# First stage of a two-layer kernel: token rows spread by a load, values in 16 columns a head, feed-forward ahead of the first rotation

## The reference, cut to what matters

```python
xn = layernorm(x)
# attention, 16 heads of 8
Q, K = rope(xn @ W_q.T), rope(xn @ W_k.T)
V = xn @ W_v.T
# feed-forward whose weights depend on the batch: tokens 1 to 16 of it
even, odd = xn[:, 1:17][:, ::2], xn[:, 1:17][:, 1::2]
m1 = (even[:, :4, :, None] * odd[:, :4, None, :]).reshape(B, 512, 128)
m2 = (even[:, 4:, :, None] * odd[:, 4:, None, :]).reshape(B, 128, 512)
h = gelu(xn @ W1.T + scale * (xn @ m1.T) + b1)
u = h @ W2.T + scale * (h @ m2.T) + b2
```

## Time and profile before

| | |
|---|---|
| median of 3 runs | 987.8 us (986.38 to 988.86) |
| the profiled execution | 987.3 us |
| its span | 985.5 us |
| mean granted clock of TensorE | 0.943 of full |
| PE, DVE, ACT, POOL busy | 88%, 81%, 74%, 29% of the span |
| first stage | up to about 121 us |

### The profile page before, as it was taken

The page is one execution under the profiler, slowest core; times in us unless marked ns, Lnnn a source line. Parts: engine busy times, 40 slices in busy tenths (PEclk is TensorE's granted clock), DMA queues, the critical chain, the costliest instruction groups (busy, mean ns, idle before and its releaser), DMA issues. The chain is left out here.

```text
span 985.5 us, 25281 instructions
## 1 busy us (share of the span) xinstructions
PE 862.6 (88%) x9414; PEld 461.0 (47%) x9414; DVE 801.8 (81%) x1697; ACT 726.1 (74%) x1493; POOL 290.6 (29%) x329
## 2 busy tenths in 40 slices
PE   3999999999999999999899899898999999899960
PEld 3666533333333333333334776543444444377750
DVE  6665899999999999999842664599999999847885
ACT  2656438888888888888876555688999999867741
POOL 4866311111111000000003676501444442014560
PEclk9999959999999999999989899879999999989985
DMA  5579681644445353330007778595544442556717
GB/s 170 200 262 338 253 210 50 209 101 113 113 102 120 86 124 77 75 67 23 14 8 185 234 243 247 138 232 117 119 110 91 99 80 47 136 187 185 225 75 255
DMA packets 119385, 140.92 MB, mean 143 GB/s; under 512 B 20109, under 2 KB 82138, under 8 KB 118624
## 3 DMA queue, kind: packets, MB, share of 16 engines
q1 hardware_dynamic: 113888, 127.45, 47.5%
q0 software_dynamic: 5376, 11.85, 4.1%
HBM read 77.63 MB, written 63.25 MB: 143 GB/s over the span
## 5 line engine op out<-in xcount | busy, mean ns | idle before, releaser
L974 ACT ACTIVATE probsB<-psB 128x512 f32<-128x512 f32 (+2 forms) x640 | 310.1, 565 | 75.9 <-PE psB L1029 49.3
L174 DVE TENSOR_REDUCE mxB<-psB 128x1 f32<-128x512 f32 x428 | 245.9, 642 | 9.2 <-PE psB L151 8.1
L1022 PE MATMUL psB<-q_groups,k_groups 64*128 64x512 bf16 (+3 forms) x768 | 206.4, 332 | 17.1 <-DVE mxB L174 8.3
L151 PE MATMUL psB<-k_groups,q_groups 64*128 64x512 bf16 (+2 forms) x740 | 205.6, 338 | 1.8 <-PEq L408 1.8
L1050 PE MATMUL psB<-probsB,vB 128*32 128x512 f32 (+3 forms) x1536 | 165.8, 504 | 0.7 <-ACT probsB L974 0.5
L1862 ACT ACTIVATE psD<-psD 128x896 f32<-128x896 f32 (+2 forms) x192 | 153.5, 800 | 9.2 <-PE psD L1916 8.7
L1022 PEld LDWEIGHTS psB<-q_groups,k_groups 64*128 64x128 bf16 x768 | 67.8, 94 | 162.7 <-ACT probsB L974 140.2
L1791 DVE TENSOR_REDUCE sumsD<-psD 128x1 f32<-128x128 f32 (+3 forms) x256 | 113.3, 482 | 7.0 <-PE psD L1939 4.9
L1916 PE MATMUL psD<-k_groups,q_groups 64*128 64x512 bf16 (+3 forms) x384 | 103.3, 343 | 14.1 <-ACT psD L1862 3.4
L174 DVE TENSOR_REDUCE mx2B<-psB 128x2 f32<-128x256 f32 (+3 forms) x188 | 102.6, 596 | 11.0 <-PE psB L158 9.5
L1029 PE MATMUL psB<-hide_laterB,chooseB 64*128 64x64 bf16 (+1 forms) x1024 | 109.8, 205 | 0.0
(11 more groups left out here) (240 smaller groups left out, 1552.5 us busy)
## 6 DMA issues: line engine op xcount, KB each, us to landing
v<-vaugA SPq DMA_DIRECT2D x4, 2048.0 KB, 8.8
vB<-v SPq DMA_DIRECT2D x16, 512.0 KB
q_groups<-q SPq DMA_DIRECT2D x32, 200.0 KB
k_groups<-k SPq DMA_DIRECT2D x32, 200.0 KB
back<-emptyB POOLq DMA_DIRECT2D x16, 256.0 KB, 3.8
q<-hiA SPq DMA_DIRECT2D x12, 256.0 KB, 6.5
k<-hiA SPq DMA_DIRECT2D x12, 256.0 KB, 5.8
q_groups<-q SPq DMA_DIRECT2D x32, 96.0 KB
```

Source lines behind the costliest of these rows:

```text
L151: ins = nc.tensor.matmul(bank[:, to:to + w], self.q[r, s, a, t * P:t * P + P], self.k[r, s, a, HALF * c:HALF * c + w], start=True, stop=(c ...
L174: return nc.vector.tensor_reduce(dst, src, AX.X, ALU.max)
L974: nc.scalar.activation(probs[:, n % DEEP, 0:w], st[n % BANKS][:, 0:w], ACT.Exp, scale=DH ** -0.5).then_inc(exp_done, 1)
L1022: ins = nc.tensor.matmul(bank[:, to:to + w], k[half[r], s, hq // 2, jt * P:jt * P + P], q[half[r], s, hq // 2, i0:i0 + w], start=True, sto ...
```

## The change

- `pick`, its load and PE's `outer` go. In `normalise`, after the second tile, ACT stores the eight rows to memory (`first`, 4 KB), and in a new step `spread_first` it waits for that and loads them back with a broadcasting access into all 128 partitions of `firstA` (512 KB written). DVE's `weights` waits for this load (`first_moved`) and reads `firstA` in SBUF where it read PSUM banks 0 and 1.
- `spread_first(0)` stands between `normalise(0)` and `columns(0)`; `spread_first(b+1)` between `second_part(b, 0)` and `second_part(b, 1)`.
- A head's values take 16 columns (`VC`) in `vaug`, `v0` and the tile of `attention`, whose products still take 32 columns: the head's own 16 and the 16 behind them. The tile gets 16 spare columns, set to zero by POOL.
- In batch 0, DVE does `weights(0)` before `rope(0, 0)`, ACT does `gelu(0, 0)` before `first_part(0, 0)`, and PE does `project(0, 1)` in the middle of `feed_forward(0, 0)`. ACT runs a small Gelu at its start.

```diff
+VC = 2 * DH
-        pick = m.sb("pickA", [P, 8, P])
+        first = m.sb("firstA", [P, 8 * D])
-        vaug = m.sb("vaugA", [P, 2, NT, H, VW])
+        vaug = m.sb("vaugA", [P, 2, NT, H, VC])
...
-        consts = [(ident, A["ident"]), (w_proj, A["w_proj0"]), (pick, A["pick"]), (cos, A["cos0"]), (sin, A["sin0"]),
+        consts = [(ident, A["ident"]), (w_proj, A["w_proj0"]), (cos, A["cos0"]), (sin, A["sin0"]),
...
-                    dve.wait_ge(outer_done, b + 1)
+                    dve.wait_ge(first_moved, 32 * (b + 1))
...
-                        V.scalar_tensor_tensor(w1e[:, c], ps[:, 0, c], odd[:, j:j + 1], w1[:, c], ALU.mult, ALU.add)
+                        V.scalar_tensor_tensor(w1e[:, c], first[:, c], odd[:, j:j + 1], w1[:, c], ALU.mult, ALU.add)
...
-                    rope(b, 0)
                     if b == 0:
                         weights(b)
+                    rope(b, 0)
...
+                        if t == 1:
+                            act.wait_ge(xn_ready, NT * b + 1)
+                            act.dma_start(A["first"][b].rearrange("o (j c) -> (o j) c", c=D), xn[1:17:2, 0, :]).then_inc(first_moved, 16)
+
+                def spread_first(b):
+                    act.wait_ge(first_moved, 32 * b + 16)
+                    if b:
+                        act.wait_ge(w_ready, b)
+                    act.dma_start(first[:, :], A["first"][b].broadcast_to((P, 8 * D))).then_inc(first_moved, 16)
...
+                act.wait_ge(ready, 1)
+                nc.scalar.activation(warm[:, :], eps[:, :], ACT.Gelu)
                 normalise(0)
+                spread_first(0)
                 columns(0)
...
                     keep_v(b)
+                    gelu(b, 0)
                     if b == 0:
                         first_part(0, 0)
-                    gelu(b, 0)
...
                     second_part(b, 0)
+                    if b + 1 < B:
+                        spread_first(b + 1)
                     second_part(b, 1)
...
+                    if b == half == 0:
+                        pe.wait_ge(terms_ready, 1)
+                        project(0, 1)
...
                 turn_rows(0)
-                outer(0)
                 pe.wait_ge(xnT_ready, 2)
                 project(0, 0)
                 values(0)
-                pe.wait_ge(terms_ready, 1)
-                project(0, 1)
...
-                        outer(b + 1)
...
-        v = m.sb("vB", [P, QUADS, NT, 4 * VW])
+        v = m.sb("vB", [P, QUADS, NT * 4 * VC + VW - VC])
...
+                nc.gpsimd.memset(v[:, :, NT * 4 * VC:], 0.0).then_inc(loaded, 1)
...
-                        ins = nc.tensor.matmul(pv[VW * hq:VW * hq + VW, HALF - w:HALF], v[:, s, jt, VW * hq:VW * hq + VW],
+                        ins = nc.tensor.matmul(pv[VW * hq:VW * hq + VW, HALF - w:HALF], v[:, s, VC * (4 * jt + hq):VC * (4 * jt + hq) + VW],
```

More of the change, by code:

```diff
@@ L373, in project_and_ffn @@
         scale = m.sb("scaleA", [P, 1])
-        pick = m.sb("pickA", [P, 8, P])
+        first = m.sb("firstA", [P, 8 * D])
         eps, power = m.sb("epsA", [P, NT]), m.sb("powA", [P, NT])
+        warm = m.sb("warmA", [P, NT])
         x = m.sb("xA", [P, NT, D])
@@ L394, in project_and_ffn @@
         projected, v_done, v_kept = m.sem("projectedA"), m.sem("v_doneA"), m.sem("v_keptA")
-        outer_done, odd_ready, w_ready = m.sem("outer_doneA"), m.sem("odd_readyA"), m.sem("w_readyA")
+        first_moved, odd_ready, w_ready = m.sem("first_movedA"), m.sem("odd_readyA"), m.sem("w_readyA")
         terms_ready, roped_ready = m.sem("terms_readyA"), m.sem("roped_readyA")
@@ L493, in weights @@
                         c = slice(j * P, j * P + P)
-                        V.scalar_tensor_tensor(w1e[:, c], ps[:, 0, c], odd[:, j:j + 1], w1[:, c], ALU.mult, ALU.add)
+                        V.scalar_tensor_tensor(w1e[:, c], first[:, c], odd[:, j:j + 1], w1[:, c], ALU.mult, ALU.add)
                     for j in range(4):
                         o = slice(j * 32, j * 32 + 32)
-                        ins = V.scalar_tensor_tensor(w2e[:, :, o], ps[:, 1, j * P:j * P + P].rearrange("p (r q) -> p q r", q=FC),
+                        ins = V.scalar_tensor_tensor(w2e[:, :, o], first[:, HALF + j * P:HALF + j * P + P].rearrange("p (r q) -> p q r", q=FC),
                                                      odd[:, 4 + j:5 + j], w2[:, :, o], ALU.mult, ALU.add)
@@ L651, in turn_rows @@
                             ins.then_inc(turned, 1)
[L653 to L657, removed]
                 def project(b, half):
@@ L793, in load_values @@
                     b, s = divmod(x, QUADS)
-                    sp.dma_start(v[:, s, :, :], A["v0"][b].rearrange("p (t f) -> p t f", t=NT)[
-                        :, :, s * 4 * VW:(s + 1) * 4 * VW]).then_inc(in_loaded[s], 16)
+                    sp.dma_start(v[:, s, 0:NT * 4 * VC].rearrange("p (t f) -> p t f", t=NT), A["v0"][b].rearrange(
+                        "p (t f) -> p t f", t=NT)[:, :, s * 4 * VC:(s + 1) * 4 * VC]).then_inc(in_loaded[s], 16)
                 def place(x):
@@ L992, in turn_over @@
                     pe.wait_ge(split, 4 * (x + 1))
-                    pe.wait_ge(loaded, 16)
+                    pe.wait_ge(loaded, 16 + 1)
                     nc.tensor.transpose(mxb[n % RING][0:64, 0:P], parts[:, x % 2, :, :].rearrange("p a r -> p (a r)"),
@@ L2380, in constants @@
     p = np.arange(P)
-    pick = np.zeros((P, 8, P))
-    for j in range(8):
-        pick[2 * j + 1, j, :] = 1.0
     row = p[:, None, None] % ROWS + ROWS * np.arange(2)[None, :, None]
@@ L2394, in constants @@
         "tables1": np.stack([cos1 * qs, sin1 * qs, cos1 * ks, sin1 * ks], axis=1).astype(np.float32),
-        "pick": pick.astype(np.float32),
         "same_head": (p[:, None] // DH == p[None, :] // DH).astype(np.float32),
@@ L2431 @@
 SCRATCH = {
-    "q0": ([B, ROWS0, H, S], BF16), "k0": ([B, ROWS0, H, S], BF16), "v0": ([B, P, NT * H * VW], F32),
+    "q0": ([B, ROWS0, H, S], BF16), "k0": ([B, ROWS0, H, S], BF16), "v0": ([B, P, NT * H * VC], F32), "first": ([B, 1, 8 * D], F32),
     "u": ([B + 1, S, D], F32), "o0": ([B, H, 2 * DH, S], F32), "rden": ([B, H, S], F32),
```

## The result

| | before | after |
|---|---|---|
| median of 20 runs each | 985.85 us | 989.95 us |
| lowest and highest | 978.16 to 991.28 | 985.32 to 996.21 |
| profiled execution, its span | 987.3, 985.5 | 988.0, 986.2 |
| end of the last `u` sum of the first stage, in the profile | 120.71 | 123.06 |
| first output tile of attention, in the profile | 151.31 | 152.11 |

The ratio of after to before is 1.0048, 95% interval 1.003 to 1.0066: slower by 0.48%, 4.7 us by the ratio and 4.1 by the medians. The times of the two profiled executions differ by 0.7 us alone; single executions of one kernel spread over more than 10 us, so totals are read from the medians, and the profiles for durations and waits at one place.

A forecast was written before the change was run, and what follows sets the result against it. PE is busy 11.43 of 12 us, but the ACT and POOL chain releases its third feed-forward product, and DVE has next to no slack at the weights. 4.7 + 1.7 - 1.6 - 0.6 = +4.2 on 987.8 gives 992.0 us, range 984.5 to 995.5.

The forecast's parts named there:

- the turns: In `weights`, DVE's steps and POOL's SBUF-reading sums each wait for the other's whole instruction: +4.7 us.
- `weights` from SBUF: DVE's eight steps, both inputs now in SBUF, delayed by POOL's sums: 1.9 us in batches 1 and 2, 0.95 in batch 3.
- Rival 1: In `weights`, DVE keeps its run of eight and POOL waits instead: 985.6 to 987.3 us, chance 0.27.
- Removing `outer`: PE, batches 1 to 3: dropping 1.78 us gains 0, as the ACT and POOL chain still releases PE; at most 2.9.
- Rival 2: First stage: the ACT and POOL chain also gives way, so removing `outer` gives up to 2.9 us: 982.7 us, chance 0.08.
- ACT's two DMA issues: Store in `normalise` and load before `second_part(b, 1)` fit ACT's idle time: 0; uncovered, up to 1.2 us a batch.
- Clock: First stage: PE's new pauses bring matmuls at half clock, one spell's worth on the path, +1.7 us.
- Batch 0: New order, with the spreading load landing at 18.5, brings `first_part(0, 1)` to 35.0 from 36.60: -1.6 us.
- Values: Attention's loads move half the bytes, halving PE's 1.23 us wait for `place`: -0.6 us, bounds 0 and 1.23.

The follow-up runs named there:

- `pool_later`: Kernel after, with POOL doing `remainder(b, 0)` after `rope(b, 1)`, so it reads no SBUF beside `weights`: 1.0016 to the kernel before.
- `bank_copy`: Kernel after, with ACT copying the spread rows from SBUF into PSUM banks 0 and 1 in batches 1 to 3, read there by DVE: 0.9999 to the kernel before.
- `gelu_first`: `pool_later` with ACT doing `gelu(b, 1)` before `second_part(b, 1)`: 0.9999 to the kernel before.
- `bank_gelu`: `bank_copy` with ACT doing `gelu(b, 1)` before `second_part(b, 1)`: 0.9962 to the kernel before.
- `outer_gelu`: `outer_back` with ACT doing `gelu(b, 1)` before `second_part(b, 1)`: 0.9939 to the kernel before.
- `after_again`: Kernel after, unedited, measured once more on the second chip: 1.0041 to the kernel before.
- `values_only`: Kernel before, with only the values in 16 columns a head: 0.9958 to the kernel before.
- `outer_back`: Kernel after, with rows spread by PE again (`pick`, `outer`, PSUM reads), batch 0 order and 16 columns kept: 0.9941 to the kernel before.

## Why the prediction was right, and where it was right by luck

992.0 was predicted from a median of 987.8, +4.2 us; measured +4.1 by the medians, +4.7 by the ratio (the kernel before has 985.85 over 20 runs, so the time itself lies 2 us under 992.0). The sign and the size were right, and the term that was put first, the turns, is there at its place. But that the sum agreed is in part luck. In the changed stages the measured terms are 5.3 for the weights, 0 for `outer`, -2.95 for batch 0 and -1.5 for the values, 0.8 us together; the rest, over 3 us, comes from a place that no term named, and takes the room of a clock term that was not paid and of two gains that were put too small.

- **`weights` from SBUF, +4.7: right in mechanism, place and size.** DVE and POOL take turns in batches 1 and 2, and in batch 3 behind `odd`; 2.09 + 2.09 + 1.12 = 5.3 us. `pool_later` takes the turns away (4.27 to 2.55), `bank_copy` the second SBUF input (2.16). Of the 5.3, 0.36 a batch is the `w2e` steps being longer without any POOL, which no row of before could show; the turns alone are the rest, 4.2, a little under the estimate. Rival 1, that DVE keeps its run, is refuted. The rule of the Trainium skill ("SBUF — State Buffer", section "Who interferes with whom") holds in both halves: two SBUF inputs wait for the whole of POOL's instruction; with one in PSUM, which I said no row isolated, `bank_copy` shows no delay at all beside the same POOL sums.
- **Removing `outer`, 0: right.** The distance from the first gelu of one half to that of the next stayed 12.5 us, since the chain through ACT and POOL held PE's third product. `gelu_first` and `bank_gelu` show that it was this cover: with `gelu` first, that distance is 11.15, and `bank_gelu` has a batch 0.8 us shorter than `outer_gelu`. Rival 2 is refuted for the change as made. In the whole program, the missing instructions seem to have cost 3 us, above.
- **ACT's two DMA issues, 0: right.** 0.63 us for the store and 0.32 for the load; the 1.20 in batch 0 stretched `normalise(0)`, in a batch that came out earlier anyway.
- **Clock, +1.7: wrong where I placed it.** In batches 1 to 3 no stretch at 0.50 occurs in the profiles of any of the seven kernels with these pauses; pauses of 1.3 to 1.8 us at full clock are followed by matmuls of the usual length (3.46 us for seven, above). Among the pauses that were counted, the one in batch 0 ahead of `project(1, 0)` is followed by such a spell in two profiles: 33.4 to 36.8 us in the kernel after, 32.9 to 39.7 in `pool_later`, none in `after_again` and the others (the kernel before had one of its own in that batch, 23.3 to 26.8). It cost little: from `first_part(0, 1)` to the first `gelu` behind it took 4.51 us in the kernel after against 4.37 in `after_again`, 0.1 us; in `pool_later`, where it took 5.66, 1.3 us. So the term was worth 0.1 here; the step that failed is one spell's worth on the path.
- **Batch 0, -1.6: right in direction, 3.07 in size.** The load landed at 17.2, not 18.5; put into my own sum, that gives 33.7 for `first_part(0, 1)`, and it ran at 33.53. The mis-sized step was the load's time. At the first `gelu` behind it 2.95 was left.
- **Values, -0.6: under-sized.** Alone they give 0.42% (0.14 to 0.70), and in the profile 1.5 us between the end of the stage and attention's first output (29.09 us in `values_only` and 29.05 in the kernel after, 30.60 before), more than my bound of 1.23, which had only the one wait of `place` in it. By the figure of the Trainium skill that I set beside it ("DMA: Bandwidth & Descriptors", table "Specifications", at least 512 bytes a transfer) the term would have been 0. No run here has chunks of 256 bytes without half the bytes, so what the chunks cost by themselves is not shown.
- **What was not foreseen: +2.7 to 3.3 at `keptD`.** It took the place of the clock term and of what batch 0 and the values gave beyond the estimate. 0.8 us at attention's first output plus 2.7 at `keptD` is 3.5 of the 4.1 to 4.7 us. A part of the rest is the wait for `place` in the second group of attention, 1.01 us before, 1.26 and 1.85 in the two profiles of the kernel after. The rest, up to a microsecond, is not placed.

## What to carry to other kernels

Before an operand moves from PSUM to SBUF, look at what GpSimd does at that time: a VectorE instruction with both inputs in SBUF waits here for whole GpSimd instructions, a run of short ones pays once for each of them, and the same run with one input in PSUM pays nothing. Work taken off a busy engine is worth only what the other chain into the same wait allows; here removing 1.8 us of TensorE work a batch was worth nothing, a changed order on ScalarE alone 0.1 us, and the two together 0.9. And when a change moves time in a stage whose source it doesn't touch, look for "issue" waits at one fixed instruction and compare the instruction counts before explaining it by what the change was meant to do.

## What the runs showed of the hardware

- DVE steps whose row is read with a stride (every fourth float, four at a time for `w2e`) took 0.37 us each from SBUF (1.48 for four), and 0.28 from PSUM (1.12); with a contiguous row from SBUF they took 0.285 (1.14).
- TensorE's pauses of 0.7, 1.3 and 1.8 us in each of batches 1 and 2 left the granted clock at 1.00. In batch 0, behind pauses of 0.7 to 1.0 us, it was 0.50 for 3.4 us in the profile of the kernel after and for 6.8 us in that of `pool_later`, and 1.00 in that of `after_again`.
- A wait with no releaser, at one instruction of TensorE, was 0.3 to 0.9 us in seven kernels and 3.5 to 4.2 in seven others, which have 48 to 90 fewer of some 9,400 matmuls, 500 us earlier in the program.
- The best of the kernels tried, `outer_gelu` and `outer_back` (0.9939 and 0.9941), keep `outer` and take only the order of batch 0 and the 16 columns; `outer_gelu` also moves `gelu`.
